# Two GpSimd drains left out at the ends of blocks, and the clears of the last stage's key and value tiles moved into its first steps

## The reference, cut to what matters

```
xn = layernorm(x)
s  = rwkv_attention(xn)                      # layer zero: scans over the tokens
g  = silu(top1_of_8_experts(xn) + xn)
x  = x + s * g
xn = layernorm(x)
s  = blocked_attention(xn) @ out_w.T + out_b # layer one: 16 heads of 8, key blocks of 64
g  = silu(attention_of_4_routed_heads(xn) @ Wo + bo)
x  = x + s * g
```

## Time and profile before

| what | value |
|---|---|
| median of three executions | 1276.95 us (1275.96 to 1278.06) |
| the profiled execution | 1267.88 us |
| its span, first to last instruction | 1266.0 us |
| layer zero's block ends, layer one's begins | 393.45 us |
| first matmul of layer one | 419.73 us |
| last store of the output issued | 1260.47 us |
| busy over the span | PE 84%, DVE 84%, ACT 67%, POOL 64% |

### The profile page before, as it was taken

How to read it: one execution, slowest core, us unless ns; L and a number is a source line. 1 busy time by engine, 2 the same in 40 slices (tenths; PEclk the granted TensorE clock), 3 DMA queues, 4 the chain that set the end, 5 groups by cost and what they waited for, 6 DMA issues and landing times. The chain is left out here.

```text
span 1266.0 us, 29224 instructions
## 1 busy us (share of the span) xinstructions
PE 1067.9 (84%) x8602; PEld 691.4 (55%) x8603; DVE 1057.7 (84%) x2232; ACT 844.2 (67%) x2114; POOL 816.2 (64%) x1143
## 2 busy tenths in 40 slices
PE   3776369999981479999999999999999999999985
PEld 2665246666651245555565555555555655565552
DVE  6789979999986378888988888888888888988871
ACT  3555347777771147777777777777777777777773
POOL 4587757677773366766766676667667766766640
PEclk9866679999996579999999999999999999999998
DMA  9511111111111223323322332233233323322310
GB/s 254 159 41 37 35 38 48 45 45 46 42 44 32 54 64 89 81 63 91 84 67 66 88 91 62 76 83 85 62 78 89 75 63 85 86 72 68 82 36 11
DMA packets 147947, 89.13 MB, mean 70 GB/s; under 512 B 73057, under 2 KB 137057, under 8 KB 147553
## 3 DMA queue, kind: packets, MB, share of 16 engines
q1 hardware_dynamic: 143712, 78.92, 24.2%
q0 software_dynamic: 4096, 8.53, 2.2%
HBM read 55.91 MB, written 31.47 MB: 69 GB/s over the span
## 5 line engine op out<-in xcount | busy, mean ns | idle before, releaser
L1426 DVE TENSOR_REDUCE bm<-PS 128x16 f32<-128x1024 f32 x256 | 312.5, 1221 | 40.5 <-PE PS L1758 37.0
L1634 ACT ACTIVATE PT<-PS 128x1024 f32<-128x1024 f32 x256 | 262.2, 1024 | 53.8 <-PE PS L1770 50.1
L1780 PE MATMUL PS<-PT,V 128*32 128x256 f32 x2048 | 137.0, 385 | 0.4 <-ACT OT L1639 0.4
L1289 POOL TENSOR_TENSOR Pr<-Pr,linv 128x512 f32<-128x512 f32 x128 | 131.3, 1037 | 5.0
L1615 ACT ACTIVATE Pr<-PS,nmf 128x256 f32<-128x256 f32 x256 | 117.5, 474 | 14.1 <-DVE nmf L1446 14.1
L1770 PE MATMUL PS<-QS,KS 51*128 51x256 bf16 x1024 | 99.9, 273 | 25.5 <-ACT PT L1634 20.5
L1286 POOL TENSOR_TENSOR linv<-lsum,minus 128x4 f32<-128x4 f32 x64 | 66.4, 1037 | 77.4 <-ACT Pr L1615 77.4
L1758 PE MATMUL PS<-KS,QS 48*128 48x256 bf16 x1024 | 100.9, 275 | 18.0 <-DVE bm L1426 16.3
L1446 DVE TENSOR_REDUCE nmf<-PS 128x4 f32<-128x1024 f32 x64 | 78.1, 1220 | 19.9 <-PE PS L1841 19.9
L391 POOL DMA_INDIRECT xs_dram<-XN,slot x64 | 67.5, 1055 | 35.4 <-issue 17.9
L1821 PE MATMUL PS<-xT,wsel 128*128 128x256 f32 x256 | 75.2, 418 | 17.3 <-DVE Kf L1420 15.2
(11 more groups left out here) (246 smaller groups left out, 2821.1 us busy)
## 6 DMA issues: line engine op xcount, KB each, us to landing
wsel<-in_qkv_w SPq DMA_DIRECT2D x128, 96.0 KB, 2.5
parts_dram<-parts SPq DMA_DIRECT2D x32, 384.0 KB, 3.0
QS<-parts_dram SPq DMA_DIRECT2D x64, 96.0 KB
KS<-parts_dram SPq DMA_DIRECT2D x64, 96.0 KB
xs_dram<-zero_t SPq DMA_DIRECT2D x1, 4752.0 KB, 26.3
xs_t<-xs_dram SPq DMA_DIRECT2D x72, 66.0 KB, 1.8
ys_dram<-ys_t SPq DMA_DIRECT2D x72, 64.0 KB, 1.6
QS<-parts_dram SPq DMA_DIRECT2D x64, 64.0 KB
```

The lines of the kernel that those rows point to most:

```text
L1289: pool.tensor_tensor(Pr[i][:, qt, :, :], Pr[i][:, qt, :, :], linv[:, i, qt, :].unsqueeze(2).broadcast_to([P, 2, SEQ]), ALU.mult).then_inc( ...
L1426: dve.tensor_reduce(bm[:, i // 2, :, 2 * (i % 2):2 * (i % 2) + 2, :].rearrange("p q r b -> p r q b"), bS.rearrange("p (r q b k) -> p r q b ...
L1634: act.activation(PT[i % 4][:, :, :], bT.rearrange("p (r k) -> p r k", r=2), ACT.Exp).then_inc(s_exp, 1)
L1780: last = pe.matmul(bC[j * VC:(j + 1) * VC, 0:SEQ], V2[q][:, kt, 4 * g + j, :], PT[(2 * g + j // 2) % 4][:, j % 2, kt * SEQ:(kt + 1) * SEQ] ...
```

## The change

Both blocks are opened with `no_gpsimd_drain=True`. In layer one the clears of KS and V2 become a function `clear(i)` on DVE: two pieces of KS[i], written as 1024 float32 words whose two halves are each the bfloat16 -1, then all of V2[i], then the ones. `clear(0)` runs before DVE's loop, `clear(1)`, `clear(2)` and `clear(3)` run in DVE's steps 1, 2 and 3, behind `route_c` and ahead of `block_max(5)`. The split of the bias moves behind `clear(1)`. POOL's small constants move behind its step 0. Waits are moved to where the cleared tiles and the bias are first used.

```diff
-        block = ctx.enter_context(nc.Block())
+        block = ctx.enter_context(nc.Block(no_gpsimd_drain=True))
...
+        MINUS_ONES = -(1.0 + 0xBF80 / 2 ** 23)
...
-        def run(eng, step):
+        def run(eng, step, setup=None):
             for t in range(B + 4):
                 step(t // NQ, t % NQ)
+                if t == 0 and setup:
+                    setup()
...
-            sp.wait_ge(s_c1, 1)
-            sp.wait_ge(s_w, 16 * 6)
...
             def load_qk(t, n, q):
+                if t < NQ:
+                    sp.wait_ge(s_c1, 3 * t + 1)
                 sp.wait_ge(s_pst[q % 2], 16 * n + 16)
...
-            for i in range(NQ):
-                pool.memset(V2[i][:, :, :, :], 0.0)
-            pool.memset(mp[:, :, :, :], 0.0).then_inc(s_c0, 1)
-            pool.memset(onesb[:, :], 1.0)
-            pool.memset(minus1[:, :], -1.0)
-            pool.memset(bo3[:, :], 0.0).then_inc(s_bo, 1)
-            pool.tensor_copy(identb[:, :], ident[:, :]).then_inc(s_c2, 1)
...
+            def setup():
+                pool.memset(mp[:, :, :, :], 0.0).then_inc(s_c0, 1)
+                pool.memset(onesb[:, :], 1.0)
+                pool.memset(minus1[:, :], -1.0)
+                pool.memset(bo3[:, :], 0.0).then_inc(s_bo, 1)
+                pool.tensor_copy(identb[:, :], ident[:, :]).then_inc(s_c2, 1)
...
-            run(pool, step)
+            run(pool, step, setup)
...
-            for i in range(NQ):
+            def clear(i):
                 for j in range(2):
-                    last = dve.memset(KS[i][64 * j + 32:64 * j + 64, :, :], -1.0)
-            last.then_inc(s_c1, 1)
-            dve.wait_ge(s_c0, 1)
-            for i in range(NQ):
-                last = dve.memset(V2[i][P - BLK:P, TB - 1, :, HD:HD + 1], 1.0)
+                    last = dve.memset(KS[i][64 * j + 32:64 * j + 64, :, :].rearrange("p h t -> p (h t)").bitcast(fp32), MINUS_ONES)
+                last.then_inc(s_c1, 1)
+                dve.memset(V2[i][:, :, :, :], 0.0).then_inc(s_c1, 1)
+                dve.wait_ge(s_c1, 3 * i + 2)
+                dve.memset(V2[i][P - BLK:P, TB - 1, :, HD:HD + 1], 1.0).then_inc(s_c1, 1)
+
+            def bias_parts():
+                dve.wait_ge(s_bo, 1)
...
+            clear(0)
             dve.wait_ge(s_w, 16 * 6)
...
-            dve.wait_ge(s_bo, 1)
...
-            dve.tensor_scalar(outb_b[:, :], outb_b[:, :], 0.5, None, ALU.mult).then_inc(s_c2, 1)
-            dve.wait_ge(s_c2, 2)
+            dve.tensor_scalar(outb_b[:, :], outb_b[:, :], 0.5, None, ALU.mult).then_inc(s_c3, 1)
+            dve.wait_ge(s_c3, 1)
...
                 if run1:
                     route_c(*batch1)
+                    if batch1[0] + 1 < NQ:
+                        clear(batch1[0] + 1)
+                    if batch1[0] == 0:
+                        bias_parts()
                 if run2:
                     block_max(*batch2, 5)
...
             def v_copy(t, n, q):
                 act.wait_ge(s_vp, t + 1)
                 if isinstance(t, int) and t < NQ:
-                    act.wait_ge(s_c2, 2)
+                    act.wait_ge(s_c1, 3 * t + 3)
...
             pe.wait_ge(s_w, 16 * 6)
-            pe.wait_ge(s_c2, 2)
-            pe.wait_ge(s_bo, 5)
+            pe.wait_ge(s_c3, 1)
+            pe.wait_ge(s_c2, 1)
...
             def routed_out(t, n, q):
+                if t == 0:
+                    pe.wait_ge(s_bo, 5)
                 pe.wait_ge(s_otf, 2 * t + 2)
```

More of the change, by code:

```diff
@@ L1009, in layer_one @@
         s_c0 = sem("l1_consts_pool")
-        s_c1 = sem("l1_consts_dve")
+        s_c1 = sem("keys_and_values_cleared")
+        s_c3 = sem("constants_scaled")
         s_c2 = sem("values_set_up")
@@ L1321, in step @@
                     head_norm(*batch2, 3)
-            run(pool, step)
+            run(pool, step, setup)
         @block.vector
         def _(dve):
-            for i in range(NQ):
+            def clear(i):
                 for j in range(2):
-                    last = dve.memset(KS[i][64 * j + 32:64 * j + 64, :, :], -1.0)
-            last.then_inc(s_c1, 1)
-            dve.wait_ge(s_c0, 1)
-            for i in range(NQ):
-                last = dve.memset(V2[i][P - BLK:P, TB - 1, :, HD:HD + 1], 1.0)
+                    last = dve.memset(KS[i][64 * j + 32:64 * j + 64, :, :].rearrange("p h t -> p (h t)").bitcast(fp32), MINUS_ONES)
[5 more added lines that the diff above has]
+                dve.wait_ge(s_bo, 1)
+                dve.tensor_copy(bo_h[:, :], bo_b[:, :]).then_inc(s_bo, 1)
+                dve.wait_ge(s_bo, 2)
+                dve.tensor_copy(bo3[0:1, :], bo_h[0:1, :])
+                dve.tensor_tensor(bo_r[:, :], bo_b[:, :], bo_h[:, :], ALU.subtract).then_inc(s_bo, 1)
+                dve.wait_ge(s_bo, 3)
+                dve.tensor_copy(bo3[32:33, :], bo_r[32:33, :])
+                dve.tensor_copy(bo_h[:, :], bo_r[:, :]).then_inc(s_bo, 1)
+                dve.wait_ge(s_bo, 4)
+                dve.tensor_tensor(bo3[64:65, :], bo_r[64:65, :], bo_h[64:65, :], ALU.subtract).then_inc(s_bo, 1)
+            clear(0)
             dve.wait_ge(s_w, 16 * 6)
```

## The result

The kernel after took 1267.99 us in the median of nine executions (1266.25 to 1270.92), the kernel before, in the same job, 1277.46 us (1275.61 to 1283.73). The ratio is 0.9923, 95% interval 0.9908 to 0.9938: 9.5 us less. The profiled executions do not show this: 1268.31 us after against 1267.88 before.

The account below looks back on a forecast made before the run. The prediction put the bound at the seam between layers: POOL's DRAIN, then DVE's setup. Gains 3.6 + 3.2 + 13.1 less losses 2.5, 7.2 and 1.5 made 8.7 us, so 1276.95 became 1268.3 us, range 1259 to 1273.5.

Parts of the forecast that it names:

- Step 1: Closing of layer zero's block: without POOL's DRAIN the release waits only for ACT, 3.6 us gained.
- Step 2: Closing at the kernel's end: the release waits for SP instead of POOL's DRAIN, 3.2 us gained.
- Rival B: Both closings: a drain only moves, or is not removed; gain 5.5 or 1.9 us; chance 0.15.
- Step 3: Start of layer one: `gated` starts 7.45 us into the block instead of 20.55, 13.1 us gained.
- three candidates: What `gated` waits for: POOL's gather to tanh (4.8 us), DVE's `clear(0)` (3.6), the weights (6.5, taken as last).
- rival C: DVE's clears: a memset is priced by bytes, each new piece costs 2.23 us, 1278.2 us in all; chance 0.06.
- Step 4: POOL's five moved instructions fit its 1.09 us idle before `inverse_std`, and moved waits hold nothing: no cost.
- Step 5: `clear(1)` and bias split in step 1: 5.1 us against 2.6 us of DVE idle time, 2.5 us lost.
- Step 6: `clear(2)` and `clear(3)` in steps 2 and 3: 3.6 us exposed twice, 7.2 us lost.
- step 7: PE's granted clock in step 3 falls after a standstill of 3.5 us, 1.5 us lost.
- A: Steps 1 to 3 hide the clears, wholly 1257.1 us, half 1262.7; chance 0.24 together with cheaper memsets.
- D: PE's clock stays low through step 3, a whole step costing 12 us, 1280.3 us in all; chance 0.05.

Follow-up runs that it names:

- e1: The kernel before, unchanged, run again: 1271.45 us, ratio 0.9993 to the kernel before in the same job.
- e3: The kernel after with both POOL drains put back, so the moved clears alone: 1269.15 us, ratio 0.9977 to before.
- e9: The kernel before with only the drain of layer one's block left out: 1268.15 us, ratio 0.9969 to before.
- e12: The kernel before, unchanged, run on one chip in one job with a copy of after: 1276.85 us, ratio 1.0003 to before.
- e8: The kernel before with only the drain of layer zero's block left out: 1268.17 us, ratio 0.998 to before.
- e2: The kernel before with both POOL drains left out and nothing else: 1265.5 us, ratio 0.9942 to before.
- e4: The kernel after with KS cleared as 2048 bfloat16 elements a piece instead of 1024 float32 words: 1269.2 us, ratio 0.9974 to before.
- e13: The kernel after, unchanged, run on one chip in one job with a copy of before: 1267.53 us, ratio 0.9933 to before.
- e10: The kernel after, unchanged, run again: 1270.62 us, ratio 0.9927 to before.
- e5: The kernel after with all four clears ahead of DVE's loop and none in the steps: 1258.51 us, ratio 0.9892 to before.
- e11: The kernel after with the clears of batches 0 to 2 ahead of DVE's loop, only batch 3's in step 3: 1265.09 us, ratio 0.9887 to before.
- e7: The kernel after with clears moved to idle places on DVE and some value clears to POOL: 1248.58 us, ratio 0.9817 to before.

## Why the prediction was right, step by step

The forecast was 8.7 us less, 1268.3 us; measured were 9.5 us (7.9 to 11.8) and 1267.99, and in the two copies of after ratios of 0.9927 and 0.9933, 9.3 and 8.6 us. The size and the account behind it hold. That forecast and median are only 0.3 us apart is luck: the times are not known to better than 2 us.

**Step 1, the first closing (3.6 us).** Right. The first load of layer one is issued at 393.6 on average in the kernels with this drain (before, e1, e3, e9, e12: 393.45, 393.00, 393.60, 394.31, 393.50; mean 393.57) and at 388.7 to 391.4 in the nine without it (mean 389.9), so 3.7 us. e8 gives 2.5 (0.6 to 4.4) by the times.

**Step 2, the last closing (3.2).** Right: from the last store to the end 5.51 us before, 2.39 after, 3.1 us, in every profile; 3.9 (2.0 to 5.8) by the times of e9. Rival B, that a drain only moves, falls with e2, e8 and e9.

**Step 3, the front (13.1).** Right in size: `gated` comes 12.9 to 13.0 us earlier. One of the three candidates was mis-sized without effect. The gather with its tanh took 7.2 us from the slot copy (389.97 to 397.20) and not 4.8; it nearly ties with the weights, with 0.28 us to spare. The shorter path I read from before had no loads of SP's beside it, which I had named as a bound. The memsets are 1.16 to 1.19 us apart as taken, and e4 shows by element; rival C, by bytes, falls.

**Step 4 (nothing).** Right: POOL's five instructions end at 400.32 and POOL still waits 0.28 us for DVE's statistics.

**Step 5, step 1 of the pipeline (2.5).** Right: 2.35 us in e13 against e12, 2.2 in the pair shown, 2.5 in e3 against e1.

**Step 6, steps 2 and 3 (7.2), and step 7, the clock (1.5).** Together 8.7. The clear is fully exposed. In step 2 it takes from the start of `route_c`'s product to the next block maximum 4.64 us in e13 and 0.96 in e12, so 3.7 us of DVE, and the step is 3.6 us longer. In step 3 DVE's part is 4.63 - 1.26 = 3.4 us and the step is 4.4 us longer.

The forecast was read from a profile in which the clock is at 1.00 through step 3. Its counterpart is e10, a copy of after that also has 1.00 there up to the clear. PE in step 3 of e10, and two stretches with PE's busy time, its granted clock, the DMA share and GB/s:

```profile
471.46 1.10 PE L1831 MATMUL PS<-xT,wsel 128*128 128x256 f32 x4
...
477.49 0.50 PE L1768 MATMUL PS<-KS,QS 48*128 48x256 bf16 x4 [3.60 <-DVE bm L1432]
...
478.51 2.07 PE L1831 MATMUL PS<-xT,wsel 128*128 128x256 f32 x4
```

```profile
474.00:476.00 2.00, 0.00 (x0) 1.00 0.68 150
...
478.00:480.00 2.00, 1.90 (x8) 0.50 0.00 0
```

This is what step 7 announced: PE stands still for 3.60 us (3.5 forecast) at the high level, the clock then falls to the low one for some 3 us, and the same four matmuls take 2.07 us where they had taken 1.10. e3 shows the same, with a standstill of 3.60 us. Set against e8, whose step 3 has no fall, step 3 of e10 is 28.05 - 23.13 = 4.9 us longer. DVE's part of it is 4.63 - 0.97 = 3.7, which leaves 1.3 us for the clock (1.5 forecast). Steps 1, 2 and 3 together lose 2.8 + 3.6 + 4.9 = 11.4 us in e10 and 11.2 in e3, against the forecast of 2.5 + 7.2 + 1.5 = 11.2. The profiles compared are of different jobs.

In other executions the clock takes another course and the price is lower: e12 has a fall in step 3 without any clear, so part of the loss is in both kernels. Steps 2 and 3 lose 8.0 us in e13 against e12 and 6.3 in e3 against e1. In e13 a second fall comes behind the clear: DVE and PE of e13 there,

```profile
469.87 0.93 DVE L1411 SCALAR_TENSOR_TENSOR gc<-gall,gsum,gscale 64x6 f32<-64x6 f32 x2
...
474.50 1.23 DVE L1432 TENSOR_REDUCE bm<-PS 128x16 f32<-128x1024 f32 x1
```

```profile
471.06 1.10 PE L1831 MATMUL PS<-xT,wsel 128*128 128x256 f32 x4
...
475.78 0.39 PE L1768 MATMUL PS<-KS,QS 48*128 48x256 bf16 x4 [2.29 <-DVE bm L1432]
...
476.81 1.79 PE L1831 MATMUL PS<-xT,wsel 128*128 128x256 f32 x4 [0.41 <-DVE Kf L1426]
```

PE stood still 2.29 us before 475.78, and the next projection took 1.79 us where the one before the standstill took 1.10: 0.7 of the remaining 1.0 us on one group; the other 0.3 is not shown. One reading in the forecast was wrong. I took the high clock of step 3 for the kernel's habit. In e12 the granted clock is 0.57 in the stretch 478 to 482, with no clear near it, and in after 0.50 from 466 on, ahead of the clear. The standstill that I announced for step 3 is therefore 1.17 us in after and 2.29 in e13; in step 2, where the clock is low anyway, it is 4.29 us in both.

The rivals: A, that steps 1 to 3 hide the clears, falls by e3, e5 and e11 (a step with a clear is longer, one without it is not, but for the clock), although such places exist, as e7 shows. D, a clock that stays low, falls: it is at 1.00 again from 474 in after and from 482 in e10 and e13.

**The bound of the method.** The forecast was made against a profiled execution 9.07 us below its median, and that distance was taken as kept. It was not: after's profiled execution is 0.3 us above its median. The forecast was right all the same, since its terms were differences of stages and took nothing from the spans. The reading that I announced, 11 us more from the first matmul to step 4, gives 9.8 us between the two profiles shown and 10.3 between e12 and e13. It depends on which executions were profiled: after against e1 it would be 7.2.

## What to carry to other kernels

A drain at a block's end costs what it takes beyond the last report of the other engines, here 3.1 to 3.6 us of 6.0 to 6.5; read that difference, not its duration, and check by taking it out alone. Work that is moved from a serial front into the pipeline's fill steps is only hidden where the engine's next instruction still shows a wait for another engine afterwards: three clears and the bias split behind `route_c` cost 9 to 11 us of the 13 gained, while at covered places they cost nothing that the stages show, and that kernel gained 23.3 us in all. Before a stage of a profile is compared with another, take a second profile of the unchanged kernel in the same job, and see where the granted clock rises and falls in each: two copies of one program differed by 5.5 us in their steady steps and by 2.5 in the fill.

## What the runs showed of the hardware

- The same program ran its 28 steady steps in 698.3 us in one job (e1) and 703.8 in another (e12), on another chip, with the granted clock at 1.00 in both; ACT's wait for PE's products of L1780 is longer in the second (13.8 against 7.1 us in the 400 from 700 to 1100). The cause is open.
- POOL's DRAIN took 6.5 us at the first closing and 6.1 at the last, and is no work put off: without it (e2, e8) POOL's first work of the next block, the four clears of L1198, takes 3.63 us as in before.
- The clock can fall in step 3 without any clear in it: in e12 to 0.57 over 478 to 482, after a stretch (474 to 478) in which PE was busy 2.56 of 4 us. The profile of before that is shown has 1.00 throughout step 3, although PE was busy only 2.13 of 4 us from 474 to 478. After a standstill of 3.60 us at 1.00 it was at 0.50 in e3 and e10.
- A DVE memset of 32 partitions by 1024 float32 and one of 128 by 1024 take the same 0.91 us, 2048 bfloat16 1.77. From start to start 1024 elements more cost 2.23 - 1.17 = 1.06 us. The Trainium skill, "VectorE: DVE Perf Modes", section "Zero memsets can be issued as uint32 (trn2)", says that a memset takes one cycle for each element whatever its type. The trace agrees in that the time goes with the elements and not with the bytes or partitions, and here this holds for a value that is not zero.
